# A message-passing network with half of its scatter as a dense product: a seventh dense pass of 256 columns, and 32 fewer gathered chunks in layers 1 to 3

## The reference, cut to what matters

```python
def _L0_gnn_ref(...):
    m = clifford_linear(h_hc[src] * r_hc[edge_type], msg_w, msg_b)   # 256x256 linear map of each edge's product
    m = m * gate[:, :, None] * norm[:, None, None]                   # gate of the relation, degrees of both ends
    h_agg = jax.ops.segment_sum(m, dst, num_segments=num_nodes)
    return clifford_linear(h_hc + h_agg, upd_w, upd_b)

def _sage_conv(x, src, dst, Wl, bl, Wr, n_nodes):
    summed = jax.ops.segment_sum(x[src], dst, num_segments=n_nodes)
    deg = jax.ops.segment_sum(jnp.ones(...), dst, num_segments=n_nodes)
    return summed / jnp.maximum(deg, 1.0)[:, None] @ Wl.T + bl + x @ Wr.T

x = _layernorm(x + _L0_gnn_ref(x, ...))
h = relu(_sage_conv(x, W1l, b1l, W1r)); h = relu(_sage_conv(h, W2l, b2l, W2r))
out = _layernorm(x + _sage_conv(h, W2l, b2l, W2r))
```

## Time and profile before

| | us |
|---|---|
| median of 3 runs (lowest, highest) | 3321.13 (3313.59, 3326.47) |
| the profiled execution | 3326.72 |
| its span, first to last instruction | 3323.2 |
| mean granted TensorE clock | 0.927 |

### The profile page before, as it was taken

How to read it: one execution, slowest core, us unless ns; L and a number is a source line. 1 busy time by engine, 2 the same in 40 slices (tenths; PEclk the granted TensorE clock), 3 DMA queues, 4 the chain that set the end, 5 groups by cost and what they waited for, 6 DMA issues and landing times. The chain is left out here.

```text
span 3323.2 us, 53365 instructions
## 1 busy us (share of the span) xinstructions
PE 2852.0 (86%) x16283; PEld 2436.2 (73%) x16283; DVE 2414.4 (73%) x5400; ACT 2130.6 (64%) x3761; POOL 2416.0 (73%) x2281
## 2 busy tenths in 40 slices
PE   5569999989899999995899999588999958899995
PEld 4458888877788778874778788477878847778784
DVE  7968888888888888885566666456666645777776
ACT  1067777777777777772677777267777726677771
POOL 5267777777777777774777777577777757777773
PEclk7579999999999999997999999789999979999997
DMA  4256656666666656665666665466666546666663
GB/s 135 75 145 169 168 157 170 167 166 166 165 167 167 163 156 167 167 165 165 198 191 189 192 191 179 150 218 188 192 190 189 180 154 208 196 198 198 206 193 91
DMA packets 327859, 572.41 MB, mean 172 GB/s; under 512 B 47877, under 2 KB 225878, under 8 KB 327574
## 3 DMA queue, kind: packets, MB, share of 16 engines
q0 software_dynamic: 105696, 290.56, 32.1%
q1 hardware_dynamic: 218361, 275.92, 26.2%
q10 hardware_dynamic: 3517, 2.48, 0.3%
HBM read 494.21 MB, written 74.56 MB: 171 GB/s over the span
## 5 line engine op out<-in xcount | busy, mean ns | idle before, releaser
L1475 POOL DMA_INDIRECT rows_arena<-table_h,src_idx x1224 | 1304.7, 1066 | 460.4 <-issue 369.9
L1475 POOL DMA_INDIRECT rows_arena<-table_scaled_x,src_idx x782 | 830.1, 1062 | 280.1 <-issue 273.6
L2038 PE MATMUL bank<-wide_counts,h_pairs 128*128 128x512 f32 x3528 | 876.1, 400 | 0.0
L2038 PEld LDWEIGHTS bank<-wide_counts,h_pairs 128*128 128x128 f32 x3528 | 661.5, 193 | 137.5 <-DVE h_pairs L1820 0.7
L1975 PE MATMUL bank<-rel_pairs,ftype_hot 125*128 125x258 f32 x4688 | 711.7, 299 | 53.5 <-ACT ftype_hot L1601 50.7
L1812 DVE TENSOR_TENSOR row_pairs<-rows_arena,row_pairs 128x1024 fp32r<-128x1024 f32 x306 | 373.5, 1221 | 450.2 <-ACT row_pairs L1610 448.5
L1975 PEld LDWEIGHTS bank<-rel_pairs,ftype_hot 125*128 125x128 f32 x4688 | 622.4, 192 | 88.6 <-ACT ftype_hot L1601 50.8
L1610 ACT CAST row_pairs<-rows_arena 128x1024 fp32r<-128x1024 f32 x306 | 320.1, 1046 | 476.5 <-DMA rows_arena<-table_h,src_idx 468.0
L1998 PE MATMUL bank<-row_pairs,rel_pairs 128*128 128x256 f32 x2448 | 392.5, 306 | 182.3 <-DVE row_pairs L1812 182.1
L1622 ACT CAST wide_counts<-rows_arena 128x1024 fp32r<-128x1024 bf16 (+1 forms) x450 | 501.9, 1115 | 0.0
L1998 PEld LDWEIGHTS bank<-row_pairs,rel_pairs 128*128 128x128 f32 x2448 | 339.3, 203 | 214.3 <-issue 209.1
(11 more groups left out here) (186 smaller groups left out, 3106.5 us busy)
## 6 DMA issues: line engine op xcount, KB each, us to landing
rows_arena<-edge_counts SPq DMA_DIRECT2D x234, 512.0 KB, 4.0
edge_counts<-fcount SPq DMA_DIRECT2D x48, 832.0 KB, 6.3
rows_arena<-in_edge_type_dram SPq DMA_DIRECT2D x195, 187.5 KB
rows_arena<-table_h,src_idx POOLq DMA_INDIRECT x1224, 3.6
rows_arena<-table_h SPq DMA_DIRECT2D x36, 512.0 KB, 12.1
rows_arena<-table_scaled_x,src_idx POOLq DMA_INDIRECT x782
table_h<-chunk_info SPq DMA_DIRECT2D x96, 128.0 KB, 4.2
rows_arena<-in_x_dram SPq DMA_DIRECT2D x6, 1024.0 KB
```

Of the source, the lines that this page charges most:

```text
L1475: pool.indirect_dma_start(out=rows[:, g % ring, c, :], out_offset=None, in_=table[:, :], in_offset=bass.IndirectOffsetOnAxis(ap=src_idx[:, ...
L2038: last = pe.matmul(bank[2 + h][:, 0:PASS_COLS], h_pairs[:, v % HALVES, part, b % HALF, h * P:(h + 1) * P], wide_counts[:, v % HALVES, b % ...
```

## The change

A seventh pass is added, of 256 columns instead of 512. The dense nodes become 6 x 512 + 256 = 3328 (3072 before), `D0` goes from 3178 to 2922 and `G0` from 102 to 94. Layers 1 to 3 gather 94 quads each (376 chunks instead of 408); 102 of the 196 quads are dense. There are 343 dense units a layer instead of 294, the 49 new ones with matmuls of 256 columns, 175 halves instead of 150, 91 tiles of counts instead of 78 (the 13 new ones of 256 KB), and 32 windows instead of 34. In layer 0, 406 chunks are counted instead of 374, over the same 392 half slots, and 52 stores of counts go out instead of 48. One scratch row of the setup now lies in parts of two others.

```diff
-PASSES, PASS_COLS = 6, 512
+PASSES, PASS_COLS, LAST_COLS = 7, 512, 256
...
     WD = PASSES
-    D0 = N - WD * PASS_COLS
+    DENSE_COLS = (WD - 1) * PASS_COLS + LAST_COLS
+    D0 = N - DENSE_COLS
...
-    STORES = WD * PASS_COLS // STORE_COLS
+    STORES = DENSE_COLS // STORE_COLS
...
+            def cols_of(w):
+
+                return PASS_COLS if w < WD - 1 else LAST_COLS
...
-            sp.dma_start(count_tile[:, t % ATILES, :, :].rearrange("p c b -> p (c b)"),
-                         counts[t // TPW, t % TPW, :, :]).then_inc(s_tile[t % ATILES], 16)
+            n = cols_of(t // TPW)
+            sp.dma_start(count_tile[:, t % ATILES, 0:n, :].rearrange("p c b -> p (c b)"),
+                         counts[t // TPW, t % TPW, :, 0:n * HTILE]).then_inc(s_tile[t % ATILES], 16)
...
-            act.copy(wide_counts[:, v % HALVES, 0:n, :],
-                     count_tile[:, t % ATILES, :, b % HTILE:b % HTILE + n].rearrange("p c b -> p b c")
+            cols = cols_of(v // HPW)
+            act.copy(wide_counts[:, v % HALVES, 0:n, 0:cols],
+                     count_tile[:, t % ATILES, 0:cols, b % HTILE:b % HTILE + n].rearrange("p c b -> p b c")
...
-                cols = agg[:, h, D0 + PASS_COLS * w:D0 + PASS_COLS * (w + 1)]
-                track(dve.tensor_tensor(cols, cols, bank[2 + h][:, 0:PASS_COLS], ALU.add))
+                cols = agg[:, h, D0 + PASS_COLS * w:D0 + PASS_COLS * w + cols_of(w)]
+                track(dve.tensor_tensor(cols, cols, bank[2 + h][:, 0:cols_of(w)], ALU.add))
...
-                    last = pe.matmul(bank[2 + h][:, 0:PASS_COLS],
+                    last = pe.matmul(bank[2 + h][:, 0:cols_of(w)],
                                      h_pairs[:, v % HALVES, part, b % HALF, h * P:(h + 1) * P],
-                                     wide_counts[:, v % HALVES, b % HALF, :],
+                                     wide_counts[:, v % HALVES, b % HALF, 0:cols_of(w)],
```

More of the change, by code:

```diff
@@ L233, in gnn_program @@
         idx_h = sb("idx_h", [P, 2, EB * P], BF16, setup)
-        check_w = {"iota_key": KEYS, "idx_f": 2 * NDP, "hi4": 2 * NDP, "chunk_pos": 2 * NDP, "chunk_far": 2 * NDP, "chunk_out": 2 * NDP, "outside": 2 * NG * GC}
+        check_w = {"iota_key": KEYS, "idx_f": 2 * NDP, "hi4": 2 * NDP, "chunk_pos": 2 * NDP, "chunk_out": 2 * NDP, "outside": 2 * NG * GC}
         assert sum(check_w.values()) <= AGGW
@@ L240, in check_part @@
             return check[:, at:at + check_w[name]].rearrange("p (a c) -> p a c", a=2)
-        idx_f, hi4, chunk_pos, chunk_far_all, chunk_out, outside = (check_part(n) for n in check_w if n != "iota_key")
-        chunk_far = chunk_far_all[0:1, :, :]
+        idx_f, hi4, chunk_pos, chunk_out, outside = (check_part(n) for n in check_w if n != "iota_key")
         real = [(P, 0, EFULL)] + ([(EREM, EFULL, EFULL + 1)] if EREM else [])
@@ L481, in _ @@
                                         ALU.mult, ALU.add))
-                step(pool.tensor_tensor(chunk_far[:, 0, 0:ND], chunk_first[0:1, 0:ND], bound, ALU.subtract))
-                step(pool.tensor_tensor(chunk_far[:, 1, 1:ND], chunk_first[0:1, 1:ND], chunk_first[0:1, 0:ND - 1],
+                step(pool.tensor_tensor(hi4[0:1, 0, 0:ND], chunk_first[0:1, 0:ND], bound, ALU.subtract))
+                step(pool.tensor_tensor(idx_f[0:1, 1, 1:ND], chunk_first[0:1, 1:ND], chunk_first[0:1, 0:ND - 1],
                                         ALU.subtract))
@@ L559, in violations @@
                                               float(HTILE * (CHUNK_W - 1)), None, ALU.is_gt)
-                    dve.tensor_scalar(chunk_row[:, 0, 0:ND], chunk_far[:, 0, 0:ND], 0.0, None, ALU.is_lt)
-                    dve.tensor_scalar(chunk_row[:, 1, 0:ND], chunk_far[:, 0, 0:ND], 2.0 * SLACK, None, ALU.is_gt)
-                    dve.tensor_scalar(chunk_row[:, 2, 1:ND], chunk_far[:, 1, 1:ND], 0.0, None, ALU.is_le)
+                    dve.tensor_scalar(chunk_row[:, 0, 0:ND], hi4[0:1, 0, 0:ND], 0.0, None, ALU.is_lt)
+                    dve.tensor_scalar(chunk_row[:, 1, 0:ND], hi4[0:1, 0, 0:ND], 2.0 * SLACK, None, ALU.is_gt)
+                    dve.tensor_scalar(chunk_row[:, 2, 1:ND], idx_f[0:1, 1, 1:ND], 0.0, None, ALU.is_le)
                     step(dve.tensor_copy(chunk_at[:, :], chunk_pos[0:1, 0, :]))
```

## The result

The changed kernel takes 3299.87 us (median of 5 runs, 3296.03 to 3303.57) against 3325.72 us (5 runs, 3313.59 to 3333.24) on the same chip: ratio 0.9927, 95% interval 0.9903 to 0.9952. It is faster, by 26 us or 0.7%. The forecast was 3263 with a range of 3225 to 3304: the time lies inside the range, near its slow end. The forecast's sum of 60.6 us less stands against 26.8 in the profiled executions (3326.7 and 3299.9).

What follows compares the result with a forecast made beforehand. POOL was taken to bound all layers, with PE late after the change. Gathers less waiting left 81.6 us; less 12 (pass ends), 6 (tail), 3 (layer 0), 60.6 us off 3326.7: 3266.1, or 3260.5 by the median; forecast 3263, range 3225 to 3304.

Steps and rivals of the forecast that it cites:

- What bounds the kernel, and what takes over: All four layers go at POOL's pace; after the change PE is late in slots 3 to 72 of layers 1 to 3.
- The 5.82 us a slot: Layer 1, slots 3 to 72: PE's work comes to 407.3 us, 5.82 a slot, against POOL's 5.48.
- the 14.6 us of waiting: Layer 3: POOL's forecast waiting, pass ends included; 10.6 us of it from PE's lateness.
- The unseen prices: Slots 73 to 83: 0.52 us per 256-column unit; pass ends: waits for `add_dense` of 4 us a layer, +12.
- PE's lateness that reaches POOL: Layers 1 to 3: beyond 13 us of free lateness, POOL waits 18.5, 20.8 and 10.6 us.
- The gathers' price: Layers 1 to 3: 32 gathers fewer each at 1.371 to 1.375 us, 131.6 us in all if POOL stays the bound.
- Layer 0: 32 more counts in layer 0 can all hide, except waits in half slots with two counts: +3 us, bounds 0 and 41.
- layer 0 gives it back: Rival: DVE is layer 0's second bound and the added counts' 41 us show, 3301 us; chance 0.06.
- Hand-overs and tail: Layer 3's end: nine blocks left instead of seven at 2.92 us each on DVE, +6; ends of layers 1 and 2: nothing.
- ACT can't feed PE: Rival, slots 3 to 72: ACT makes halves too late; 0.29 us more a dense slot cancels the gain; chance 0.11.
- POOL as the bound: Rival, layers 1 to 3: PE keeps up and POOL still sets the pace, 3204 us or 3198 against the median; chance 0.08.

Runs made afterwards that it cites:

- the run with half the matmuls: Changed kernel with the second (low part of h) of the two dense matmuls a block and half left out: 3243.24 us, ratio 0.9736 to before.
- the kernel with paired counts: Kernel before with 14 of its 374 chunk counts moved one place forward, so 14 places carry two: 0.9985 on the first kind, 1.0025 and 1.0016 on slower chips.
- the kernel with both retunings: Changed kernel with the last pass ending 6 quads before the last gather instead of 10, and six work tiles instead of five: 3249.88 us, ratio 0.9762 to before.

## Why the prediction was right, and where not

*What bounds the kernel, and what takes over.* Right for layers 1 and 2. All layers of before went at POOL's pace, and in passes two to six PE took over, busy 248 of 250 us at clock 1.00, without the 3.86 us wait and the dip of the clock behind a pass that the earlier trace rows has. The 5.82 us a slot are near: from slot 3 to 72 the `row_lows` came 5.97 us apart in layer 1, 5.95 in layer 2 and 5.84 in layer 3. In layer 3 the step failed: POOL's own four gathers took 5.68 us a slot there, so PE fell hardly behind POOL, and of the 14.6 us of waiting only 0.9 came.

*The unseen prices.* Right. The units of 256 columns, bounded by 0.46 and 0.92 us and taken as 0.52, are 20.6 / 160 = 0.129 us a matmul, 0.52 a unit; and PE waited for `add_dense` 4.8 us in layer 1 where I took 4:

```profile
L2044 PE MATMUL bank<-wide_counts,h_pairs 128*128 128x256 f32 x160 | 20.6, 282 | 1.1 <-DVEq L1839 1.1
```

```profile
PE bank L2044 <- DVEq L1839: 4.8, 5, 1.8
```

*PE's lateness that reaches POOL.* Right in kind, as the run with half the matmuls shows, but twice too large: 61.9 us with the pass ends, 30.9 measured. POOL's waits fell at quads 49 to 74, as foreseen. The lateness was worked out against gathers at 1.371 us; at the measured 1.40 to 1.42 POOL itself needs 5.6 to 5.7 us a slot instead of 5.48, so less is left to wait for. This miss and the next one cancel for three quarters. That the phases came within 10.8 us of the forecast is partly luck.

*The gathers' price.* This is the step that failed in the layers. I priced 376 gathers at before's mean, 1.371 us; they took 1.406, 1.397 and 1.420 us without their waits, 41.7 us more in all, and 20.8 us more even in the run where PE holds nothing. A mean is not a gather's own price: that is 0.945 us, the 0.3 between two, and what one loses when it starts inside a DVE instruction with two inputs in SBUF. DVE carries more halves a slot in the changed kernel, and both `row_lows` and the `h_pairs` subtractions fell less well for the gathers. The row to read was the timeline of POOL beside DVE.

*Layer 0.* The largest single miss of the sum: +3 taken, +16 measured, within my bounds of 0 and 41. The term took it that all of the counting hides, but for the waits in the places with two counts. One such wait, at the very first place, alone cost POOL 5.4 us: POOL waits for its first ring place there in any case, so nothing hides it. And I did not ask how far behind POOL its consumers stand, which comes back at the layer's end: 5.8 of 7.8 us. The rival "layer 0 gives it back" named the place and put 0.06 on it.

*Hand-overs and tail.* The tail's two blocks are right; waits for the load of a work tile and for PE were left out, +5.5. The hand-overs, costed at nothing, are +4.6; with other block orders they are 23.3 to 28.1 us, so they hang on what the order leaves there; what in it was not looked into.

*The rivals.* That ACT can't feed PE fell with the first profile, and for good with half the matmuls. POOL as the bound is what that run shows, and even it needs 3243 us, not 3204: the rival had the same price for a gather.

*The stated time.* Of the 33.8 us by which the sum missed, 10.8 are the layers' phases (41.7 of dearer gathers less 31.0 of waiting that did not come), 13.1 layer 0, 4.6 the hand-overs and 5.5 the tail.

## What to carry to other kernels

A mean duration holds the contention of its stretch. Before multiplying it by a count, split it into the shortest case and what overlap adds, and ask whether the change moves the overlap. When work is added to engines that hide behind the bound, look not only for the bound's waits but at the lag of the consumers: a stage's end pays the lag even if the bound never waits. And after a change of the bound, retune what was set for the old one; here the end of the last pass and one more buffer were worth twice the change itself.

## What the runs showed of the hardware

A gather on POOL takes 0.945 us alone. One that starts within a DVE instruction with both inputs in SBUF, of 128x1024, 128x512 or 128x256, ends 0.82 us after that instruction; in two kinds of DVE adds with one input in PSUM none of 57 was held. Cutting the 128x1024 subtraction into two of 128x512 makes the mean gather 0.054 to 0.058 us shorter.

The second kind of chip was not expected. There PE is held in stretches of some 10 us, with nothing that the trace shows as a releaser. PE in layer 2 of the kernel with paired counts on it, start and us, and then busy time by stretch:

```profile
2268.28 1.30 PE L2039 MATMUL bank<-wide_counts,h_pairs 128*128 128x512 f32 x2 [1.51 <-issue]
...
2270.40 1.01 PE L2039 MATMUL bank<-wide_counts,h_pairs 128*128 128x512 f32 x2 [0.81 <-issue]
...
2271.78 0.58 PE L2039 MATMUL bank<-wide_counts,h_pairs 128*128 128x512 f32 x1 [0.38 <-issue]
...
2273.19 0.79 PE L2039 MATMUL bank<-wide_counts,h_pairs 128*128 128x512 f32 x1 [0.82 <-issue]
```

```profile
2240.00:2262.00 22.00, 19.87 (x98) 16.49 (x97) 8.20 (x14) 9.71 (x14) 17.13 (x17) 0.97 0.49 157
2262.00:2277.00 15.00, 7.56 (x16) 4.12 (x16) 4.12 (x8) 3.68 (x7) 8.32 (x9) 0.61 0.27 83
2277.00:2300.00 23.00, 23.00 (x117) 19.75 (x116) 15.49 (x28) 16.89 (x25) 12.23 (x12) 0.96 0.54 160
```

16 matmuls in 15 us, against 98 in the 22 us ahead. ACT, DVE and in the end POOL (9.16 us) wait behind them. In this profile 64 idle times of over 0.3 us stand ahead of a dense matmul without a releaser, 64.5 us together; the eight profiles from the first kind of chip have none. Between such stops a dense matmul takes the same there, 0.231 us from start to start against 0.230. What holds PE was not found, nor whether it explains the whole of the 15 to 18% by which before is slower there. Comparisons of a few microseconds on these chips tell little, nor do they carry over: the split made before 2.5% slower there, while on the first kind it took 21 us off the kernel with both retunings. Before with the split, the changed layer 0 alone and the changed layers alone were not run on the first kind.
